# Waiting for every three transfers of the sorted-edge scatter in a graph network kernel

## The reference

```python
x = layernorm(x + gru_layers(x))      # 3 times: agg = segment_sum((h @ W)[src], dst); h = GRU(agg, h)
x = layernorm(x + hypergraph(x))      # two segment sums, weights by degree, batch norm, relu
x = layernorm(x + attention(x))       # softmax over the edges of a source node
x = layernorm(x + edge_mlp(x))        # per edge MLP of (x[src], x[dst]), segment_sum at dst, node MLP
```

## Time and profile before

| | value |
|---|---|
| timed median of 3 runs | 4749.77 us (4746.3 to 4755.25) |
| span of the profiled execution | 7303.0 us |
| PE busy | 4076.2 us, 56% |
| DVE busy | 3381.7 us, 46% |
| POOL busy | 2658.9 us, 36% |
| ACT busy | 2340.3 us, 32% |
| mean granted TensorE clock | 0.754 |

### The profile page before, as it was taken

The page is one execution under the profiler, slowest core; times in us unless marked ns, Lnnn a source line. Parts: engine busy times, 40 slices in busy tenths (PEclk is TensorE's granted clock), DMA queues, the critical chain, the costliest instruction groups (busy, mean ns, idle before and its releaser), DMA issues. The chain is left out here.

```text
span 7303.0 us, 82736 instructions
## 1 busy us (share of the span) xinstructions
PE 4076.2 (56%) x24237; PEld 3354.5 (46%) x24238; DVE 3381.7 (46%) x7886; ACT 2340.3 (32%) x3120; POOL 2658.9 (36%) x2706
## 2 busy tenths in 40 slices
PE   4332641019981111117989798988672197666655
PEld 2111420007761101106778586858571197665644
DVE  4222540358970000106788776456451076555545
ACT  0000010005640000004555455557461075444433
POOL 4555157730017777770000000000427601444463
PEclk7665865559995555558999898989785598888777
DMA  9400000009970000116658287843444343444432
GB/s 376 155 0 0 0 2 0 0 23 334 368 250 0 0 0 0 28 25 222 232 189 293 96 293 214 296 162 95 132 125 124 97 139 98 132 132 130 130 95 67
DMA packets 364823, 923.20 MB, mean 126 GB/s; under 512 B 114026, under 2 KB 138716, under 8 KB 364531
## 3 DMA queue, kind: packets, MB, share of 16 engines
q1 hardware_dynamic: 214722, 650.09, 26.9%
q10 hardware_dynamic: 58609, 180.13, 6.4%
q0 software_dynamic: 91200, 89.42, 5.2%
HBM read 705.69 MB, written 213.71 MB: 126 GB/s over the span
## 5 line engine op out<-in xcount | busy, mean ns | idle before, releaser
L1741 POOL DMA_INDIRECT edges_halves<-local,gather_idx x832 | 854.9, 1027 | 791.7 <-SPq L372 505.4
L1680 POOL DMA_INDIRECT adj_t<-cell_val,cell_at x832 | 828.6, 996 | 465.2 <-issue 369.9
L862 PE MATMUL ps<-tiles_r,stage_r 128*128 128x512 f32 x2028 | 811.6, 400 | 158.2 <-issue 132.0
L1134 POOL DMA_INDIRECT big<-table,gather_idx x576 | 548.4, 952 | 832.3 <-DVE stage L1284 376.3
L869 PE MATMUL ps<-stage,big 128*128 128x130 f32 x4046 | 520.1, 284 | 370.3 <-issue 354.7
L1134 POOL DMA_INDIRECT x_fm<-table,gather_idx x384 | 370.2, 964 | 959.8 <-DMA table<-cell_at 689.7
L869 PEld LDWEIGHTS ps<-stage,big 128*128 128x128 f32 x4046 | 497.9, 199 | 388.5 <-issue 384.6
L2059 PE MATMUL ps<-big,ident_h 128*128 128x104 bf16 (+1 forms) x2880 | 359.7, 256 | 460.4 <-issue 459.7
L1253 PE MATMUL ps<-big,stage 128*128 x1920 | 356.2, 342 | 352.7 <-issue 189.3
L1319 PE MATMUL ps<-ident,big 128*128 128x128 f32 x260 | 73.3, 377 | 817.2 <-issue 768.2
L2442 DVE TENSOR_TENSOR big<-ps,stage 128x1248 bf16<-128x1248 f32 x192 | 270.7, 1451 | 519.5 <-remote 385.1
(11 more groups left out here) (482 smaller groups left out, 9007.8 us busy)
## 6 DMA issues: line engine op xcount, KB each, us to landing
onehot<-adj_t SPq DMA_DIRECT2D x332, 512.0 KB
big<-adj_t SPq DMA_DIRECT2D x332, 512.0 KB
onehot<-adj_s SPq DMA_DIRECT2D x170, 512.0 KB
adj_t<-rows ACTq DMA_DIRECT2D x13, 6656.0 KB
adj_s<-big ACTq DMA_DIRECT2D x157, 512.0 KB, 5.3
stage<-local_rows SPq DMA_DIRECT2D x120, 512.0 KB
big<-adj_s SPq DMA_DIRECT2D x84, 512.0 KB
x_fm<-adj_s SPq DMA_DIRECT2D x84, 512.0 KB
```

The costliest lines, as they stand in the source:

```text
L862: nc.tensor.matmul(psum_fm(p, n)[:, 0:cut], upper_rows[:, k, :], tile[:, 0:cut], start=k == 0, stop=False, skip_group_check=True)
L1134: return nc.gpsimd.indirect_dma_start(out, None, table[0:N, :], bass.IndirectOffsetOnAxis(gather_idx[:, t:t + 1], 0))
L1680: nc.gpsimd.indirect_dma_start(out, bass.IndirectOffsetOnAxis(cells[:, c:c + 1], 0), cell_val[:, c:c + 1], None).then_inc(S(name), 16)
L1741: nc.gpsimd.indirect_dma_start(edges_halves, bass.IndirectOffsetOnAxis(slot_at[:, at:at + 1], 0), slot_val[:, at:at + 1], None).then_inc(h ...
```

## The change

A constant is added, and in the loop of L1741 a wait on POOL behind each third transfer of a slab: it holds POOL until all transfers of this slab so far have landed.

```diff
+SORTED_TOGETHER = 3
...
                     nc.gpsimd.indirect_dma_start(edges_halves, bass.IndirectOffsetOnAxis(slot_at[:, at:at + 1], 0),
                                                  slot_val[:, at:at + 1], None).then_inc(halves_written[n % 2].sem, 16)
+                    if (c + 1) % SORTED_TOGETHER == 0:
+                        wait(pool, halves_written[n % 2], 16 * (SLW * (n // 2) + c + 1))
```

## The result

The changed kernel takes 5182.36 us (median of 4 runs, 5175.7 to 5185.26) where the kernel before takes 4750.75 us (4 runs, 4746.3 to 4755.25). The ratio is 1.0911, with a 95% interval of 1.0895 to 1.0926: 432 us slower. The forecast was slower, by 130 us. The sign and the place were right and the size was not.

A forecast was written before the change was run, and what follows sets the result against it. PE in the GRU steps and matrix passes was taken to bound the timed stretch, 1282 us, with the scatter hidden beside it; 272 waits make it late by (211 + 43) / 2 = 127 us: 4749.8 + 127, rounded 4880 us, range 4690 to 5200.

The forecast's parts named there:

- The place and the payment: At the gather of the pairs and DVE's `pair_keys`: a late scatter is paid in full, 127 us.
- The time that POOL has: From the scatter's start: it may end 1319 us later without harm, 37 us of that before DVE needs the pairs.
- The time of a transfer: In POOL's scatter: 0.97 us busy each, with the middle between a gap of 0.30 us and none.
- The landing: Behind each third scatter transfer: POOL idle 2.04 us, taken from the end of the first scatter, 272 times.
- The estimate from the Trainium skill: Waits in the streamed part of the scatter: HBM access at high load adds up to 1.8 us each, 490 us in all.
- Hidden: Rival for the scatter's end: quicker transfers and landings finish it within 1319 us, 4750 us; chance 0.25 with the no-effect rival.
- Faster: Rival for engines beside the scatter: up to 190 us of stall is real and partly goes, 4560 to 4700 us; chance 0.17.
- Much later: Rival for waits in passes 1 to 3: 3.5 us idle each, scatter late by 610 us, 5360 us; chance 0.12.
- The stall: Engines beside POOL's scatter: 1054 us of stall come with recording each instruction, none in the timed runs.

The follow-up runs named there:

- disturbed trace: First profile of the unchanged kernel, recorded ahead of the prediction; nothing was edited; its span is 7303.0 us.
- Thirteen together: Against the changed kernel, POOL waits behind each thirteenth transfer instead of each third, 64 waits: 4742.28 us, ratio 0.9994 to the kernel before.
- Before, undisturbed: Second profile of the kernel before, with no edit; its span is 4745.0 us.
- the wait on the triple before: Against the changed kernel, triples alternate between two semaphores and POOL waits for the preceding triple: 4739.52 us, ratio 0.9988 to the kernel before.

## Why the prediction was wrong

**The place and the payment: right.** The scatter is late, DVE stands in `pair_keys`, and the lateness is paid in full: 450 us of waiting, less the 8 us that the others gained and 4 us ahead of "first", is the 438 us between the spans.

**The time that POOL has: right.** 1319 us were predicted from stretches of the disturbed trace. DVE was ready 1346 us after the scatter's start, and the gather of the pairs took 12 us from its first issue: 1334 us. Thirteen together confirm it from below: POOL reached that gather 1332 us after the scatter's start, and DVE did not wait.

**The time of a transfer: too short.** The sum took the middle between a gap of 0.30 us and none. Before, undisturbed, has the 0.30 us in an execution as long as the timed ones, so it is real: 560 gaps × 0.15 = 84 us. The transfer's 0.97 us is a median; beside streams it is busy for 1.02 us and more, 855 us in all for 807: 48 us. One argument for the middle was that 1.20 us were the most that the timed run allowed; it took pass 0 (506 us) to follow the first scatter, as in the disturbed trace. In before, undisturbed, its products run from 693.8 to 1216.7 us, mostly beside that scatter (86.7 to 1170.3 us), so the bound meant nothing; without the waits the scatter of this change took 1117 / 832 = 1.34 us for a transfer.

**The landing: the step that failed.** "I take 2.04 us for the landing, the row of the same kind" mis-sized it: it measured 757.4 / 272 = 2.78 us, 202 us more in all. 84 + 48 + 202 = 334 us, and the predicted 1446 us of scatter plus 334 are 1780, for 1785 measured to the start of the pairs' gather. It was late by 1785 − 1334 = 451 us where 127 were predicted. The 2.04 us was no flat price but one point, and of a slightly different wait: the last wait of a scatter, ahead of a gather, is 1.97 us in the changed kernel too, with nothing streaming. Within the scatter it is 1.46 us alone, and 4.2, 4.2 and 3.8 us in passes 1, 2 and 3 (157.3 / 37, 159.2 / 38, 137.0 / 36). I wrote that the row was measured with the engines idle and that the stream would cost 272 us for each further us, but took the landing beside the stream at the idle value. Some two thirds of the predicted scatter lay beside a stream, and it should have been priced between 2.04 and the 7.1 us of the earlier trace rows. The stream itself was read too low as well: 217 GB/s and a share of 0.64 are means over a GRU step and a pass, while the passes alone show 274 to 293 GB/s and 0.83 to 0.88. The estimate from the Trainium skill, "DMA: Bandwidth & Descriptors", section "Latency and other measured facts" (2 us of HBM latency at high load for 0.2), added 1.8 us to a wait beside a stream; the traces show 2.8 us more there in passes 1 and 2 and 2.4 in pass 3. Its 490 us in all counted that for all 272 waits, also for those outside a stream.

**Rivals.** *Hidden* came true for 64 waits and for the wait on the triple before, not for 272. *Faster*: the part of the stall that it allowed was not there, and the scatter's real cost to the others is 13 to 21 us. *Much later* took 3.5 us for each wait and 610 us of lateness; it had the right cause, the stream, and came out 160 us above the 450, since it took every wait as if beside a stream. The measured 2.78 us are a mean of both kinds.

**The stall.** It was right that the timed runs of this kernel don't have it. It was wrong that it "comes with recording each instruction": the second profile of the same kernel was recorded just so and does not have it. For the same reason the changed kernel's profile did show the lateness, which I had said it would hide.

## What to carry to other kernels

A wait behind every few transfers costs one uncovered landing each time, so price it at the landing beside the traffic that will really run there, and if a bound on what is in flight is wanted, wait for the group before the last one: here a bound of 3 to 6 cost nothing, and gained nothing either. An engine far off the critical path has a budget: this one had some 220 us before its next hand-over was late, and 64 waits just fitted in it, 136 and 272 did not. When a profile is far longer than the timed runs, take a second profile before pricing anything from it.

## What the runs showed of the hardware

- The landing of a scatter of 128 elements of four bytes to DRAM, seen from the end of its issue: 1.46 us quiet; 3.8 to 4.3 us on average beside a stream of some 280 GB/s with three in flight, and 3.9 us with one; 11 to 24 us beside the store of `degree_row`, 26 KB in some 6650 packets, which keeps the DMA engines busy at 1 GB/s.
- The stall of the earlier trace rows, 1.40 us for each PE instruction while POOL issued, was in one profiled execution of this kernel and not in the other. Its cause stays open: no later trace holds it.
- 832 scatters beside three GRU steps and three matrix passes cost the other engines 13 to 21 us of 1310.
